# Output biases of five stages added by VectorE, and the expert biases in the middle of the last stage

## The chip, the core and the metric

One core of one Trainium2 chip runs the whole program. The metric is the device time of one execution in microseconds (us), the median of several runs. TensorE (PE) multiplies, with its weight loads shown apart (PEld); VectorE (DVE), ScalarE (ACT) and GpSimd (POOL) work on vectors; SyncE (SP) issues the transfers (DMA). Engines run their own instructions in order and wait for each other by semaphores.

## The reference

Four pre-norm layers over x of 2048 tokens x 128, in f32: eight stages, each of the form x = x + stage(layernorm(x)). Five of them matter here:

```python
# layer 0, attention: 16 heads of 8
q, k, v = split(x @ Wqkv.T + bqkv)
x = x + softmax(q k^T / sqrt(8)) v @ Wo.T + bo
# layer 0, feed-forward
x = x + gelu(h @ w1 + b1) @ w2 + b2
# layer 2, attention over three neighbouring tokens
x = x + out @ Wo.T + bo
# layer 3, feed-forward: eight experts, two per token, and a shared one
oe = silu((h @ w1 + b1) * (h @ w3 + b3)) @ w2 + b2      # per expert
x = x + sum(rw * oe) + (hs @ sw2 + sb2)
```

`bv` (the part of `bqkv` for v), `bo`, `b2`, `bo` and `sb2` are vectors of 128 that are added to every token. The expert biases `b2` of layer 3 (8 x 128) are weighted by the routing weights of the token.

## The kernel before

The running x lies in SBUF as `X`, 128 partitions x 16 tiles x 128: a token is a partition of a tile. Work goes in four chunks of four tiles (512 tokens; `NC`, `TPC`, `CW`). Every stage begins with a norm stage (VectorE normalizes tile by tile, TensorE transposes into `xnT`), during which SyncE issues the stage's weight loads. Each stage is a block: its engines start together and the next block starts when all are done.

A product whose result has tokens on partitions and features along the row can't take its bias from ScalarE's per-partition operand. The kernel before adds such a bias with a TensorE product over one row: `ones[0:1, 0:P]` (one partition of ones) times the bias row `[1, D]`, accumulated into the same PSUM tile. That is one such product for each of 16 tiles in each of five places:

- `l0_attend`, tasks of the kind "v" (L335, L336): the values of four chunks, written to PSUM `l0s_mx`, a ring of four buffers that also holds the maximum products (`max`, L346), the query and key products (`qk`, L331) and the output transposes (`ot`). ScalarE copies a values chunk from the ring to `V` (`fill_v`, L424); VectorE reduces the maximum products (L478). The table `DENSE0` puts chunk 0 ahead of the score loop and chunks 1 to 3 in its rounds 2, 3 and 4. A round is four scores (L362), four maximum products and sixteen value products (L376); there are 256.
- `token_major_out` (l0o; L581, L582): the output projection of the first attention. VectorE adds each chunk to `X` (L595) and computes the moments for the next norm (L156, L159), with the root steps (L168, L129 to L137) after the third and the fourth chunk.
- `l0_ffn` (l0f; L635 the bias, L637 four products): the downward product of a tile.
- `l2_attention` (l2a; L1250, L1251): the output projection, chunk by chunk between the score products (L1222), with one PSUM buffer `l2a_po`; VectorE adds at L1315.
- `l3_ffn` (l3f): here both kinds of bias come at the very end, for four chunks, in `biases(c)`: the expert biases as a product over eight rows (`maskT` times `b2`, L1643), the shared one over one row (L1644). They use the ring `l3f_dn` of two PSUM buffers, as the downward products of the experts do (L1634), which VectorE adds with the routing weight as its factor (L1767), or without one for the shared expert and the biases (L1763). The transposed routing weights `maskT` are made in the middle, behind groups 6, 8, 10 and 12 (`TURNED_AT`).

Of the kernel before, what the change touches and what calls it, by code (L numbers as in the profile page):

```python
# [10 lines left out]
ALU = mybir.AluOpType  # L11
# [4 lines left out]
P = 128  # L16
D = 128
# [51 lines left out]
def row_of(vector):  # L69

    return vector.rearrange("(a n) -> a n", a=1)

# [184 lines left out]
def l0_attend(nc, ctx, W, norm, xnT, vals, ident, ones, V, QS, KS):  # L257
# [38 lines left out]
    v_set, v_done = sem("v_set"), sem("v_done")  # L296
# [23 lines left out]
    with nc.Block() as block:  # L320
        @block.tensor
        def _(pe):
            def mx_task(key):
# [74 lines left out]
        def _(act):  # L398
# [22 lines left out]
            def fill_v(i):  # L421
                n = slot[("v", i)]
                act.wait_ge(mx_full, n + 1)
                nc.scalar.activation(V[:, TPC * i:TPC * (i + 1), :, 0:HD0],  # L424
                                     mx[:, n % MX0, :].rearrange("p (t j c) -> p t j c", t=TPC, c=HD0),
                                     ACT.Copy).then_inc(v_done, 1)
                act.wait_ge(v_done, i + 1)
                act.sem_inc(mx_free[n % MX0], 1)

# [6 lines left out]
            def fills(r):  # L436
                for kind, i in DENSE0.get(r, []):
                    if kind == "qk":
                        fill(i)
                    else:  # L440
                        fill_v(i)
# [4 lines left out]
            act.wait_ge(v_set, 2)  # L446
# [16 lines left out]
        def _(dve):  # L463
# [86 lines left out]
def token_major_out(nc, ctx, tag, W, w_dram, b_dram, vals, X, ident, ones, used, moments):  # L550
# [3 lines left out]
    bo = sb("bo", [1, D])  # L554
# [4 lines left out]
    transposed, copied, done, added = sem("transposed"), sem("copied"), sem("done"), sem("added")  # L559
    with nc.Block() as block:  # L560
        @block.sync
        def _(sp):
            sp.dma_start(Wo[:, :], w_dram).then_inc(loaded.sem, 16)
            sp.dma_start(bo[:, :], row_of(b_dram)).then_inc(loaded.sem, 16)
# [8 lines left out]
        def _(pe):  # L573
# [17 lines left out]
        def _(dve):  # L591
            for c in range(NC):
                dve.wait_ge(done, TPC * (c + 1))
# [10 lines left out]
def l0_ffn(nc, W, norm, X, xnT, ones, moments):  # L604

    NB = F0 // P
    with ExitStack() as ctx:
# [4 lines left out]
        b2 = sb("b2", [1, D])  # L612
        loaded = W["loads"].stage(4)

        def load(sp):
# [3 lines left out]
            sp.dma_start(b2[:, :], row_of(W["L0_ffn_b2"])).then_inc(loaded.sem, 16)  # L619
# [5 lines left out]
        up_done, act_done, dn_done, added = sem("up_done"), sem("act_done"), sem("dn_done"), sem("added")  # L625
        with nc.Block() as block:
            @block.tensor
            def _(pe):
                pe.wait_ge(loaded.sem, loaded.all)

                def down(c):
                    pe.wait_ge(act_done, NB * (c + 1))
                    for t in range(TPC * c, TPC * (c + 1)):
                        o = dn[:, c, (t % TPC) * D:(t % TPC + 1) * D]
                        nc.tensor.matmul(o, ones[0:1, 0:P], b2[0:1, :], start=True, stop=False)  # L635
                        for b in range(NB):
                            last = nc.tensor.matmul(o, hT[:, b, t * P:(t + 1) * P], w2[:, b, :],  # L637
                                                    start=False, stop=(b == NB - 1))
# [23 lines left out]
            def _(dve):  # L662
                for c in range(NC):
                    dve.wait_ge(dn_done, c + 1)
# [480 lines left out]
def l2_attention(nc, W, norm, X, xnT, ident, ones, moments):  # L1145
# [6 lines left out]
    with ExitStack() as ctx:  # L1152
# [4 lines left out]
        bo = sb("bo", [1, D])  # L1157
# [4 lines left out]
        def load(sp):  # L1162
# [4 lines left out]
            sp.dma_start(bo[:, :], row_of(W["L2_attn_bo"])).then_inc(loaded.sem, 16)  # L1167
# [22 lines left out]
        o_done, po_full, po_read = sem("o_done"), sem("po_full"), sem("po_read")  # L1190
# [1300 lines left out]
```

## Time and profile before

| | before |
|---|---|
| median of 3 runs | 3157.16 us (3152.45 to 3158.06) |
| profiled execution | 3151.58 us |
| its span, first to last instruction | 3149.8 us |
| TensorE busy | 2954.1 us, 94% |
| VectorE busy | 2210.3 us, 70% |
| ScalarE busy | 1419.3 us, 45% |
| mean granted clock of TensorE | 0.910 of 2.4 GHz |

Busy time is that of the whole program, over stages with different limits; the rows further down are from the places of the change. The granted clock has two levels, 1.0 (2.4 GHz) and 0.5 (1.2 GHz).

### The profile page before, as it was taken

To read this page: it belongs to the slowest core of one execution; us is meant where nothing else is said; L and a number is where in the kernel's file an instruction comes from. 1 tells how busy PE (TensorE), PEld (TensorE's weight loads), DVE (VectorE), ACT (ScalarE), POOL (GpSimd) and SP (SyncE) were. 2 spreads that over 40 slices of the span, in tenths; PEclk is the share of its full clock that TensorE was granted. 3 is DMA by queue.
4 is the path that set the end of the run, shared out by engine and by line. 5 is a ranking of instruction groups with operands and counts; after the bars stand their busy time and mean duration, and the time that the engine had idled before them with its cause. 6 is when DMAs were issued, how large, how long until landed. Compare 5 with 4: busy or idle time off the path is not lost. (4 is left out here: it accounts for less than half of the span.)

```text
span 3149.8 us, 43331 instructions
## 1 busy us (share of the span) xinstructions
PE 2954.1 (94%) x15864; PEld 1838.4 (58%) x15864; DVE 2210.3 (70%) x4583; ACT 1419.3 (45%) x2681; POOL 734.6 (23%) x608
## 2 busy tenths in 40 slices
PE   4999999999987999999999999999999787789799
PEld 2666666666654555555555555555554444556587
DVE  5788888888724877777877777777774637777554
ACT  1666666666641344444444444444444210322343
POOL 1000000000000244444444444444444100055200
PEclk7999999999987899999999999999999867555598
DMA  4112122121004011111111111111100100000000
GB/s 96 26 26 51 29 49 45 33 51 21 1 8 121 1 41 41 41 41 31 38 27 28 41 41 41 41 38 31 35 20 1 37 1 9 3 1 2 16 1 14
DMA packets 42128, 95.91 MB, mean 30 GB/s; under 512 B 12502, under 2 KB 31676, under 8 KB 32188
## 3 DMA queue, kind: packets, MB, share of 16 engines
q1 hardware_dynamic: 41916, 93.14, 13.0%
q8 instruction: 126, 2.06, 0.3%
q14 instruction: 86, 0.70, 0.1%
HBM read 35.18 MB, written 7.34 MB: 13 GB/s over the span
## 5 line engine op out<-in xcount | busy, mean ns | idle before, releaser
L957 ACT ACTIVATE l1a_PT<-l1a_st 128x512 f32<-128x512 f32 x1024 | 597.1, 598 | 759.6 <-PE l1a_st L873 755.5
L974 DVE TENSOR_REDUCE l1a_m<-l1a_aux 128x1 f32<-128x512 f32 x1024 | 667.6, 685 | 125.3 <-PE l1a_aux L835 123.1
L478 DVE TENSOR_REDUCE l0s_mquad<-l0s_mx 128x1 f32<-128x512 f32 x1024 | 635.5, 684 | 169.3 <-PE l0s_mx L346 169.3
L924 POOL TENSOR_TENSOR l1a_acc<-l1a_acc,l1a_PT 128x1024 f32<-128x1024 f32 x224 | 570.0, 2545 | 680.5 <-ACT l1a_PT L957 680.5
L454 ACT ACTIVATE l0s_PT<-l0s_st 128x512 f32<-128x512 f32 x1024 | 529.2, 601 | 236.0 <-PE l0s_st L362 232.6
L886 PE MATMUL l1a_ov<-l1a_PT,l1a_V 128*64 128x512 f32 x2048 | 495.7, 605 | 0.0
L871 PE MATMUL l1a_st<-l1a_QA,l1a_KA 128*128 128x512 f32 x1024 | 447.1, 437 | 2.4 <-issue 2.3
L362 PE MATMUL l0s_st<-l_QS,l_KS 128*128 128x512 f32 x1024 | 437.4, 430 | 3.6 <-ACT l0s_PT L454 3.5
L346 PE MATMUL l0s_mx<-l_KS,l_QS 120*128 120x512 f32 x1024 | 415.9, 412 | 20.4 <-DMA l_KS<-qk_rows 20.4
L873 PE MATMUL l1a_st<-l1a_QB,l1a_KB 65*128 65x512 f32 x1024 | 405.6, 396 | 0.0
L835 PE MATMUL l1a_aux<-l1a_KA,l1a_QA 128*128 128x512 f32 x1024 | 398.5, 437 | 0.8 <-DVE l1a_lo L986 0.8
L346 PEld LDWEIGHTS l0s_mx<-l_KS,l_QS 120*128 120x128 f32 x1024 | 328.5, 321 | 64.8 <-DMA l_KS<-qk_rows 22.0
L1022 DVE TENSOR_TENSOR l1a_acc<-l1a_acc,l1a_PT 128x1024 f32<-128x1024 f32 x224 | 272.7, 1217 | 91.0 <-ACT l1a_PT L957 91.0
L835 PEld LDWEIGHTS l1a_aux<-l1a_KA,l1a_QA 128*128 128x128 f32 x1024 | 200.7, 196 | 176.7 <-DVE l1a_m L974 82.0
L376 PE MATMUL l0s_ov<-l0s_PT,l_V 128*32 128x256 f32 x4096 | 274.1, 385 | 0.0
L886 PEld LDWEIGHTS l1a_ov<-l1a_PT,l1a_V 128*64 128x64 f32 x2048 | 124.2, 136 | 239.4 <-issue 177.6
L362 PEld LDWEIGHTS l0s_st<-l_QS,l_KS 128*128 128x128 f32 x1024 | 195.5, 192 | 114.2 <-ACT l0s_PT L454 87.1
L871 PEld LDWEIGHTS l1a_st<-l1a_QA,l1a_KA 128*128 128x128 f32 x1024 | 193.8, 189 | 109.5 <-issue 62.1
L913 POOL MEMSET l1a_KB<- 1x4096 f32 x1 | 3.5, 3504 | 942.9 <-POOLq L195 942.9
L873 PEld LDWEIGHTS l1a_st<-l1a_QB,l1a_KB 65*128 65x128 f32 x1024 | 193.6, 189 | 47.4 <-issue 13.4
L376 PEld LDWEIGHTS l0s_ov<-l0s_PT,l_V 128*32 128x32 f32 x4096 | 106.8, 109 | 103.9 <-issue 52.6
L1009 DVE SCALAR_TENSOR_TENSOR top_X<-l1a_aux,l1a_rinv,top_X 128x128 f32<-128x128 f32 x256 | 71.8, 344 | 54.5 <-PE l1a_aux L858 54.5
(348 smaller groups left out, 2763.7 us busy)
## 6 DMA issues: line engine op xcount, KB each, us to landing
l1a_KA<-l1a_hi SPq DMA_DIRECT2D x32, 512.0 KB, 7.9
l_QS<-qk_rows SPq DMA_DIRECT2D x64, 192.0 KB
l_KS<-qk_rows SPq DMA_DIRECT2D x64, 192.0 KB
l1a_QA<-l1a_hi SPq DMA_DIRECT2D x16, 512.0 KB, 4.5
l1a_QA<-l1a_lo SPq DMA_DIRECT2D x16, 512.0 KB, 8.6
l1a_QB<-l1a_hi SPq DMA_DIRECT2D x16, 512.0 KB, 4.5
l1a_KB<-l1a_lo SPq DMA_DIRECT2D x16, 512.0 KB, 6.4
qk_rows<-l0s_hi SPq DMA_DIRECT2D x64, 64.0 KB, 7.0
```

The costliest lines, as they stand in the source:

```text
L346: last = nc.tensor.matmul(o, q[:, tile, :], KS[r, h % BUF0, c * CW:(c + 1) * CW], start=True, stop=True)
L362: nc.tensor.matmul(st[:, b % ST0, :], KS[:, h % BUF0, kt * P:(kt + 1) * P], QS[:, h % BUF0, q:q + CW], start=True, stop=True).then_inc(st_ ...
L376: last = nc.tensor.matmul(ov[32 * q:32 * (q + 1), u % 2, :], V[:, u // 2, 2 * n + e, :], PT[:, (2 * r + e) % PT0, q // 2, at], start=(n == ...
L454: nc.scalar.activation(PT[:, g % PT0, b % 2, :], st[:, b % ST0, :], ACT.Exp).then_inc(exp_done, 1)
L478: nc.vector.tensor_reduce(mquad[:, u % 2, tile, g:g + 1], mx[:, n % MX0, :], axis=AX.X, op=ALU.max).then_inc(mx_free[n % MX0], 1)
L835: last = nc.tensor.matmul(o, QA[:, h % 3, q * P:(q + 1) * P], KA[:, h % 3, c * CW:(c + 1) * CW], start=True, stop=True)
L871: nc.tensor.matmul(st[:, u % ST1, :], KA[:, h % 3, kt * P:(kt + 1) * P], QA[:, h % 3, qc * CW:(qc + 1) * CW], start=True, stop=False)
L873: last = nc.tensor.matmul(st[:, u % ST1, :], KB[:, h % 2, kt * P:(kt + 1) * P], QB[:, h % 2, qc * CW:(qc + 1) * CW], start=False, stop=True)
L886: last = nc.tensor.matmul(ov[HD1 * (qc % 2):HD1 * (qc % 2) + HD1, qc // 2, :], V[:, h // 2 % 2, kt, HD1 * (h % 2):HD1 * (h % 2) + HD1], PT ...
L924: nc.gpsimd.tensor_tensor(acc[:, h % 2, 1, :], first, PT[:, g % PT_SLOTS, :], ALU.add).then_inc(added_pool, 1)
L957: nc.scalar.activation(PT[:, g % PT_SLOTS, (u % 2) * CW:(u % 2 + 1) * CW], st[:, u % ST1, :], ACT.Exp, scale=1.0 / float(np.sqrt(HD1))).th ...
L974: nc.vector.tensor_reduce(m4[:, b, q, c:c + 1], src, axis=AX.X, op=ALU.max).then_inc(aux_read, 1)
```

## The change

The bias tiles of the five places become `[128, 128]`, loaded with the row repeated over all partitions (64 KB in place of 0.5 KB each), and the one-row products go. In four stages VectorE adds the bias tile to `X` itself, four adds of 128x512 at the beginning of the stage's block (`add_bias`), before it adds the products. For the values, the evacuation of the PSUM ring moves from ScalarE to VectorE, which adds the bias tile in the same instruction and frees the buffer; it stands in VectorE's order where the chunk stands among the tasks. VectorE waits for the memset of `V` and for the bias load ahead of its first reduction. The expert biases become blocks of their own, of four 8-row products, in the groups 7, 9, 11 and 13 of the last stage.

```diff
+def add_bias(nc, X, bias, biased):
+    for c in range(NC):
+        x = X[:, TPC * c:TPC * (c + 1), :]
+        nc.vector.tensor_tensor(x, x, bias[:, :].unsqueeze(1).broadcast_to([P, TPC, D]), ALU.add).then_inc(biased, 1)
...
-    bv = sb("bv", [1, D])
+    bv = sb("bv", [P, D])
...
-        sp.dma_start(bv[:, :], row_of(W["L0_attn_bv"])).then_inc(b_loaded, 16)
+        sp.dma_start(bv[:, :], row_of(W["L0_attn_bv"]).broadcast_to([P, D])).then_inc(b_loaded, 16)
...
-                        nc.tensor.matmul(o[:, t * D:(t + 1) * D], xnT[:, at], Wt[:, 2, :], start=True, stop=False)
-                        last = nc.tensor.matmul(o[:, t * D:(t + 1) * D], ones[0:1, 0:P], bv[0:1, :],
-                                                start=False, stop=True)
+                        last = nc.tensor.matmul(o[:, t * D:(t + 1) * D], xnT[:, at], Wt[:, 2, :], start=True, stop=True)
...
-                        pe.wait_ge(v_done, u // (2 * TPC) + 1)
+                        n_v = slot[("v", u // (2 * TPC))]
+                        pe.wait_ge(mx_free[n_v % MX0], n_v // MX0 + 1)
...
             split_low(0)
+            dve.wait_ge(b_loaded, 32)
+            dve.wait_ge(v_set, 2)
...
+                elif kind == "v":
+                    dve.wait_ge(mx_full, n + 1)
+                    nc.vector.tensor_tensor(V[:, TPC * i:TPC * (i + 1), :, 0:HD0],
+                                            mx[:, n % MX0, :].rearrange("p (t j c) -> p t j c", t=TPC, c=HD0),
+                                            bv[:, :].rearrange("p (j c) -> p j c", c=HD0).unsqueeze(1)
+                                            .broadcast_to([P, TPC, J0, HD0]), ALU.add).then_inc(mx_free[n % MX0], 1)
...
-                nc.tensor.matmul(o, vT[:, t * P:(t + 1) * P], Wo[:, :], start=True, stop=False)
-                nc.tensor.matmul(o, ones[0:1, 0:P], bo[0:1, :], start=False, stop=True).then_inc(done, 1)
+                nc.tensor.matmul(o, vT[:, t * P:(t + 1) * P], Wo[:, :], start=True, stop=True).then_inc(done, 1)
...
+            dve.wait_ge(loaded.sem, loaded.all)
+            add_bias(nc, X, bo, biased)
             for c in range(NC):
+                dve.wait_ge(biased, c + 1)
                 dve.wait_ge(done, TPC * (c + 1))
...
-                        nc.tensor.matmul(o, ones[0:1, 0:P], b2[0:1, :], start=True, stop=False)
...
-                        nc.tensor.matmul(o, oT[:, t * P:(t + 1) * P], Wo[:, :], start=True, stop=False)
-                        last = nc.tensor.matmul(o, ones[0:1, 0:P], bo[0:1, :], start=False, stop=True)
+                        last = nc.tensor.matmul(o, oT[:, t * P:(t + 1) * P], Wo[:, :], start=True, stop=True)
...
-            downs_of[g] = range(len(downs), len(downs) + len(experts))
-            downs += [(y, c) for y in experts]
+            mine = [(y, c) for y in experts]
+            if g - 1 in TURNED_AT:
+                mine.append((N3, TURNED_AT.index(g - 1)))
+            downs_of[g] = range(len(downs), len(downs) + len(mine))
+            downs += mine
...
+                    if x == N3:
+                        pe.wait_ge(mt_read, c + 1)
                     for j in range(TPC):
                         o = dn[:, d % 2, j * D:(j + 1) * D]
+                        if x == N3:
+                            last = nc.tensor.matmul(o, maskT[:, TPC * c + j, :], b2[:, :], start=True, stop=True)
+                            continue
...
-                pe.wait_ge(mt_read, NC)
-                for c in range(NC):
-                    biases(c)
```

What stands in the engines' queues, at three places. TensorE before, from the first maximum products of the first attention over the values chunk 0 (in such rows `l_KS` and `l_QS` are keys and queries, `xN` a repetition):

```order
L346 MATMUL l0s_mx<-l_KS,l_QS 128x512 x28
L335 MATMUL l0s_mx<-l0s_W,top_xnT 128x128
L336 MATMUL l0s_mx<-l0s_bv,top_ones 128x128
L335 MATMUL l0s_mx<-l0s_W,top_xnT 128x128
L336 MATMUL l0s_mx<-l0s_bv,top_ones 128x128
```

The two products take turns four times. The same place on TensorE after the change, where line numbers have moved:

```order
L351 MATMUL l0s_mx<-l_KS,l_QS 128x512 x28
L342 MATMUL l0s_mx<-l0s_W,top_xnT 128x128 x4
L351 MATMUL l0s_mx<-l_KS,l_QS 128x512 x8
L338 MATMUL l0s_mx<-top_xnT,l0s_W 128x512 x2
L351 MATMUL l0s_mx<-l_KS,l_QS 128x512 x4
```

Four 128-row products stand in a row, and the one-row products are gone. VectorE at the beginning of l0o before the change (after the last work of the attention itself):

```order
L496 TENSOR_TENSOR l0a_vals<-l0s_mx,l0s_rden 128x2x4x8
L320 UNCONDITIONAL_BRANCH
L590 UNCONDITIONAL_BRANCH
L595 TENSOR_TENSOR top_X<-l0o_po,top_X 128x512
L156 BN_STATS top_stats<-top_X 128x6 x4
```

And VectorE at that place after it:

```order
L498 TENSOR_TENSOR l0a_vals<-l0s_mx,l0s_rden 128x2x4x8
L327 UNCONDITIONAL_BRANCH
L592 UNCONDITIONAL_BRANCH
L78 TENSOR_TENSOR top_X<-top_X,l0o_bo 128x512 x4
L600 TENSOR_TENSOR top_X<-l0o_po,top_X 128x512
L163 BN_STATS top_stats<-top_X 128x6 x4
```

Four adds out of SBUF have come ahead of the first add of a product; the rest of the stage is as it was. TensorE in a middle group of the last stage after the change, behind the upward products (`l3f_ab`) of group 8:

```order
L1635 MATMUL l3f_ab<-l3f_xl,l3f_wh 128x512
L1651 MATMUL l3f_dn<-l3f_w,l3f_hT 128x128 x16
L1648 MATMUL l3f_dn<-l3f_b,l3f_maskT 128x128 x4
L1673 MATMUL l3f_mt<-top_ident,l3f_mask 8x128 x4
L1635 MATMUL l3f_ab<-l3f_xh,l3f_wh 128x512
```

The line with `l3f_maskT` is a block of expert biases, which before stood, with the one-row products, behind the last downward product of the program.

## Rows read from the trace of the kernel before

**Rows 1.** The page, its first line.

```profile
span 3149.8 us, 43331 instructions
```

**Rows 2.** Busy us (instructions) by stretch: PE, PEld, DVE, ACT, POOL; clock; DMA; GB/s.

```profile
200.00:880.00 680.00, 678.31 (x5263) 467.14 (x5261) 540.62 (x931) 460.95 (x900) 0.00 (x0) 1.00 0.15 33
...
2540.00:2620.00 80.00, 58.85 (x150) 35.02 (x148) 30.72 (x92) 3.45 (x7) 0.00 (x0) 0.50 0.00 0
```

**Rows 3.** Timeline of the last 28 us: start, duration, engine, line, operation.

```profile
3124.15 7.31 PE L1634 MATMUL l3f_dn<-l3f_w,l3f_hT 128*128 128x128 f32 x64
...
3131.39 0.48 PE L1643 MATMUL l3f_dn<-l3f_b,l3f_maskT 8*128 8x128 f32 x2
3131.49 1.13 DVE L1767 SCALAR_TENSOR_TENSOR top_X<-l3f_dn,l3f_mask,top_X 128x128 f32<-128x128 f32 x4 [0.66 <-PE l3f_dn L1634]
...
3134.56 0.63 PE L1643 MATMUL l3f_dn<-l3f_b,l3f_maskT 8*128 8x128 f32 x2
...
3134.98 0.63 PE L1644 MATMUL l3f_dn<-l3f_sb,top_ones 1*128 1x128 f32 x2
...
3143.33 0.69 DVE L1763 TENSOR_TENSOR top_X<-l3f_dn,top_X 128x512 f32<-128x512 f32 x1 [2.72 <-PE l3f_dn L1644]
```

**Rows 4.** Timeline of TensorE, values chunk 1 of the first attention.

```profile
91.50 0.48 PE L336 MATMUL l0s_mx<-l0s_bv,top_ones 1*128 1x128 f32 x2
91.91 0.49 PE L335 MATMUL l0s_mx<-l0s_W,top_xnT 128*128 128x128 f32 x2
```

**Rows 5.** Timeline of TensorE, the first downward tile of l0f.

```profile
933.54 0.48 PE L635 MATMUL l0f_dn<-l0f_b,top_ones 1*128 1x128 f32 x2
933.95 1.16 PE L637 MATMUL l0f_dn<-l0f_w,l0f_hT 128*128 128x128 f32 x8
935.04 0.48 PE L635 MATMUL l0f_dn<-l0f_b,top_ones 1*128 1x128 f32 x2
```

**Rows 6.** Timeline around values chunk 0 of the first attention.

```profile
63.95 0.77 PE L335 MATMUL l0s_mx<-l0s_W,top_xnT 128*128 128x128 f32 x2
...
69.71 4.22 PE L346 MATMUL l0s_mx<-l_KS,l_QS 120*128 120x512 f32 x8
...
70.57 2.48 DVE L478 TENSOR_REDUCE l0s_mquad<-l0s_mx 128x1 f32<-128x512 f32 x4 [4.90 <-PE l0s_mx L346]
```

**Rows 7.** Timeline of l0o: first product, VectorE's chunks, its last instruction.

```profile
894.29 0.49 PE L581 MATMUL l0o_po<-l0o_Wo,l0o_vT 128*128 128x128 f32 x2
...
897.73 0.69 DVE L595 TENSOR_TENSOR top_X<-l0o_po,top_X 128x512 f32<-128x512 f32 x1 [5.58 <-PE l0o_po L582]
...
899.24 0.36 DVE L159 BATCH_NORM_AGGREGATE top_mv<-top_stats 128x2 f32<-128x6 f32 x4
...
908.99 0.69 DVE L595 TENSOR_TENSOR top_X<-l0o_po,top_X 128x512 f32<-128x512 f32 x1 [3.91 <-PE l0o_po L582]
...
912.13 0.17 DVE L137 SCALAR_TENSOR_TENSOR top_rstd<-top_work 128x12 f32<-128x12 f32 x1
...
917.96 0.16 DVE L137 SCALAR_TENSOR_TENSOR top_rstd<-top_work 128x4 f32<-128x4 f32 x1
```

**Rows 8.** Timeline at the start of the first attention.

```profile
30.59 0.53 POOL L505 MEMSET l_V<- 128x256 f32 x1
...
48.83 9.66 DVE L478 TENSOR_REDUCE l0s_mquad<-l0s_mx 128x1 f32<-128x512 f32 x16 [18.12 <-PE l0s_mx L346]
```

**Rows 9.** Timeline of l2a, six multiplications of 128x512 out of SBUF.

```profile
2531.75 3.70 DVE L1297 TENSOR_TENSOR l2a_prod<-l2a_q,l2a_k 128x512 f32<-128x512 f32 x6
```

**Rows 10.** DMA issues: KB each, median us from issue to landing.

```profile
l1a_bo<-in_L_attn_bo SPq DMA_DIRECT2D x1, 64.0 KB, 7.6
```

**Rows 11.** Timeline of l2a, output projection of chunk 0.

```profile
2558.63 0.79 PE L1250 MATMUL l2a_po<-l2a_Wo,l2a_oT 128*128 128x128 f32 x2
...
2564.42 5.30 PE L1222 MATMUL l2a_sc<-l2a_same_head,l2a_prod 128*128 128x16 f32 x24
2564.52 0.69 DVE L1315 TENSOR_TENSOR top_X<-l2a_po,top_X 128x512 f32<-128x512 f32 x1 [12.96 <-PE l2a_po L1251]
```

More of the change, by code:

```diff
@@ L295, in l0_attend @@
     heads_in = [sem(f"heads_in{i}") for i in range(BUF0)]
-    v_set, v_done = sem("v_set"), sem("v_done")
+    v_set = sem("v_set")
     m_done, m_placed = sem("m_done"), [sem(f"m_placed{i}") for i in range(2)]
@@ L553, in token_major_out @@
     Wo = sb("Wo", [P, D])
-    bo = sb("bo", [1, D])
+    bo = sb("bo", [P, D])
     vT = sb("vT", [P, S])
@@ L559, in token_major_out @@
     transposed, copied, done, added = sem("transposed"), sem("copied"), sem("done"), sem("added")
+    biased = sem("biased")
     with nc.Block() as block:
@@ L563, in _ @@
             sp.dma_start(Wo[:, :], w_dram).then_inc(loaded.sem, 16)
-            sp.dma_start(bo[:, :], row_of(b_dram)).then_inc(loaded.sem, 16)
+            sp.dma_start(bo[:, :], row_of(b_dram).broadcast_to([P, D])).then_inc(loaded.sem, 16)
             sp.wait_ge(loaded.sem, loaded.all)
@@ L611, in l0_ffn @@
         b1 = sb("b1", [P, NB])
-        b2 = sb("b2", [1, D])
+        b2 = sb("b2", [P, D])
         loaded = W["loads"].stage(4)
@@ L618, in load @@
             sp.dma_start(w2[:, :, :], W["L0_ffn_w2"].rearrange("(n p) d -> p n d", p=P)).then_inc(loaded.sem, 16)
-            sp.dma_start(b2[:, :], row_of(W["L0_ffn_b2"])).then_inc(loaded.sem, 16)
+            sp.dma_start(b2[:, :], row_of(W["L0_ffn_b2"]).broadcast_to([P, D])).then_inc(loaded.sem, 16)
         norm(load)
@@ L625, in l0_ffn @@
         up_done, act_done, dn_done, added = sem("up_done"), sem("act_done"), sem("dn_done"), sem("added")
+        biased = sem("biased")
         with nc.Block() as block:
@@ L634, in down @@
                         o = dn[:, c, (t % TPC) * D:(t % TPC + 1) * D]
-                        nc.tensor.matmul(o, ones[0:1, 0:P], b2[0:1, :], start=True, stop=False)
                         for b in range(NB):
                             last = nc.tensor.matmul(o, hT[:, b, t * P:(t + 1) * P], w2[:, b, :],
-                                                    start=False, stop=(b == NB - 1))
+                                                    start=(b == 0), stop=(b == NB - 1))
                     last.then_inc(dn_done, 1)
@@ L662, in _ @@
             def _(dve):
+                dve.wait_ge(loaded.sem, loaded.all)
+                add_bias(nc, X, b2, biased)
                 for c in range(NC):
+                    dve.wait_ge(biased, c + 1)
                     dve.wait_ge(dn_done, c + 1)
@@ L1156, in l2_attention @@
         Wo = sb("Wo", [P, D])
-        bo = sb("bo", [1, D])
+        bo = sb("bo", [P, D])
         same_head = sb("same_head", [P, P])
@@ L1189, in l2_attention @@
         p_done, tp_full, tp_read, dve_order = sem("p_done"), sem("tp_full"), sem("tp_read"), sem("dve_order")
[L1190 removed]
+        o_done, po_full, po_read, biased = sem("o_done"), sem("po_full"), sem("po_read"), sem("biased")
         XP, K, Q, V = range(4)
@@ L1286, in _ @@
                 dve.wait_ge(loaded.sem, loaded.all)
+                add_bias(nc, X, bo, biased)
                 for c in range(NC):
@@ L1313, in add @@
                     dve.wait_ge(po_full, c + 1)
+                    dve.wait_ge(biased, c + 1)
                     x = X[:, TPC * c:TPC * (c + 1), :].rearrange("p t d -> p (t d)")
@@ L1549, in l3_ffn @@
         b2 = sb("b2", [E8, D])
-        sb2 = sb("sb2", [1, D])
+        sb2 = sb("sb2", [P, D])
         expert_no = sb("expert_no", [P, E8])
@@ L1587, in l3_ffn @@
         ab_full, gate_done, z_done, h_done = sem("ab_full"), sem("gate_done"), sem("z_done"), sem("h_done")
-        dn_full, dn_read = sem("dn_full"), sem("dn_read")
+        dn_full, dn_read, shared_bias = sem("dn_full"), sem("dn_read"), sem("shared_bias")
         high_done, low_done = sem("high_done"), sem("low_done")
         groups = [(E8, c) for c in range(NC)] + [(2 * p, c) for p in range(PAIRS3) for c in range(NC)]
+        TURNED_AT = (6, 8, 10, 12)
         units, unit_of, downs, downs_of = [], {}, [], {}
@@ L1606, in block_before @@
         def block_before(d, c):
-            return max([i for i in range(d) if (downs + [(N3, k) for k in range(NC)])[i][1] == c], default=None)
+            return max([i for i in range(d) if downs[i][1] == c], default=None)
         with nc.Block() as block:
@@ L1635, in down @@
                                                     start=(i == 0), stop=(i == 1))
-                    last.then_inc(dn_full, 1)
-                def biases(c):
-                    d = len(downs) + c
-                    pe.wait_ge(dn_read, d - 1)
-                    for j in range(TPC):
-                        o = dn[:, d % 2, j * D:(j + 1) * D]
-                        nc.tensor.matmul(o, maskT[:, TPC * c + j, :], b2[:, :], start=True, stop=False)
-                        last = nc.tensor.matmul(o, ones[0:1, 0:P], sb2[0:1, :], start=False, stop=True)
                     last.then_inc(dn_full, 1)
@@ L1716, in _ @@
                 dve.wait_ge(loaded.sem, loaded.all)
+                add_bias(nc, X, sb2, shared_bias)
                 def wide(t):
@@ L1760, in add @@
                         dve.wait_ge(dn_read, before + 1)
+                    else:
+                        dve.wait_ge(shared_bias, c + 1)
                     if x >= E8:
@@ L1780, in _ @@
                     add(d, *downs[d])
-                for c in range(NC):
-                    add(len(downs) + c, N3, c)
 DM = 32
```

16 lines of the change are left out of this document (2 added, 14 removed).

## The prediction, made before the change was run

> **What bounds the kernel now.** I read the page first, then the clock and busy time by stretch, then the timeline of each of the five places that the diff touches, since a share of busy time over 3149.8 us says nothing of 25 us in one stage. The profiled execution took 3151.58 us, 1.8 around its span [rows 1]; the median of the three runs is 3157.16, 5.6 above it. In the long middle of the first attention TensorE is busy 678.3 of 680 us at the full clock [rows 2], so time that TensorE saves ahead of it moves everything behind it earlier. The reader should see in the rows one thing above all: what a one-row product costs beside a product over 128 rows.
>
> **The price of a bias product.** Every f32 product of 128 columns stands as two records. At the full clock (2.4 GHz), products of one shape follow each other every (3131.39 - 3124.15)/32 = 0.226 us [rows 3]; one change of shape lies in these 32, so I use 0.223. Where 128-row and one-row products take turns, each takes 0.41 us [rows 4], the 128-row ones too. In the feed-forward stage a bias product takes 933.95 - 933.54 = 0.41 and the four 128-row ones behind it 1.09, against 4 x 0.223 = 0.89 [rows 5]. So a change between a 128-row and a one-row product costs about 0.19 us in either direction, and a removed bias product gives back 0.223 + 2 x 0.19 = 0.61 us. At 1.2 GHz a product in turns takes (69.71 - 63.95)/8 = 0.72 us [rows 6], and one that follows its like 3134.98 - 3134.56 = 0.42 [rows 3] (8 rows and one row, which do not disturb each other); I use 0.43, so a change costs 0.29 there. That is the choice that makes this forecast: the 0.19 and 0.29 go away with the bias products, they are not a property of the 128-row product.
>
> The Trainium skill puts this as a rule in TensorEngine Tiling (Array Packing), Key Properties: changing the tiling mode (a product over at most 32 rows has one of its own) drains TensorE. It gives no figure. By its rule the extra 0.19 goes and the sum is the one below, 3104.8; without it the extra stays, which is rival 1, 3116.
>
> **First attention, values (four chunks).** Chunk 0 runs at 1.2 GHz: eight products, 5.76 us [rows 6]. Left are four at 0.43, with seven of eight changes gone: 5.76 - 4 x 0.43 - 0.29 = 3.8 us saved. VectorE sat idle 4.9 us for it [rows 6]; it now adds the bias itself (one PSUM read of 128x512, 0.69 us by the adds in [rows 7]), which fits into that idle time. Chunks 1 to 3 run at the full clock in a stretch where TensorE has no gaps [rows 4]: each loses 4 x 0.223 + 7 x 0.19 = 2.2 us, together 6.7. ScalarE's copy goes to VectorE, whose four reductions take 2.48 us [rows 6] of a round that the eight products had made 8 x 0.41 = 3.3 us longer. VectorE now waits at its start for the memset of the V tile and the bias load; the memset's last part starts at 30.59 and VectorE's first reduction at 48.83 after 18.1 us idle, behind a DMA [rows 8]: cost nothing, and if that cover were gone, the wait would be paid in full. **A: 10.5 us.**
>
> **First attention, output projection (l0o).** VectorE's chain: TensorE's first product at 894.29, first add at 897.73, end of the stage's chain at 917.96 + 0.16 = 918.12 [rows 7]. TensorE gives it 32 products. After the change it has 16, which even at 1.2 GHz take 16 x 0.43 = 6.9 us. So what is late next is VectorE: four bias adds of 128x512 out of SBUF, 3.70/6 = 0.62 us each [rows 9], 2.5 us, then two chunks of 899.24 + 0.36 - 897.73 = 1.9 us and two with the root steps of 912.13 + 0.17 - 908.99 = 3.3 us [rows 7]: 894.3 + 2.5 + 10.4 + 0.2 for hand-overs = 907.4. The bias load now writes 64 KB over 128 partitions in place of 0.5 KB, and both engines wait for it. Bounds of its delay: nothing, and the whole 7.6 us from issue to landing that a load of this same form took behind larger ones [rows 10]. Only 64 KB stand ahead of it here, so I take 0.4. End at 907.8. **B: 10.3 us.** It does not depend on the price of a change of rows.
>
> **First feed-forward (l0f).** Sixteen tiles of 1.50 us (933.54 to 935.04) [rows 5] become four products of 0.223 each, 0.89. TensorE has no gap there, and VectorE's adds lie far behind it. 16 x 0.61. The four SBUF adds (2.5 us) stand at the start, where VectorE has nothing to do until the first tiles are down. **C: 9.7 us.**
>
> **Third attention (l2a).** The whole stretch is at clock 0.50 [rows 2]. For each chunk TensorE starts the projection at 2558.63, VectorE waits 12.96 us and adds at 2564.52, 5.89 later [rows 11]; everything behind is VectorE's work and what waits for it. After: three products at 0.43, and from the last one's start to VectorE's what it was, 5.89 - 7 x 0.72 = 0.8: 2.1, so VectorE starts 3.8 earlier, and the products behind it 2564.42 - 2558.63 - 4 x 0.43 = 4.07. 3.9 on the chain, four chunks. **D: 15.6 us.** The bias adds stand ahead of VectorE's first read of the ring, in idle time.
>
> **Last feed-forward (l3f).** After the last expert add, at 3131.49 + 1.13 = 3132.62, the four bias blocks run until 3143.33 + 0.69 = 3144.02 [rows 3]: 11.4 us go from the end. Four blocks of four 8-row products come into the middle, each 4 x 0.223 + 2 x 0.19 = 1.28 us on a TensorE that has almost no gaps, 5.1 together. VectorE's share, one add of 0.69, lies beside them: an expert block takes TensorE 1.81 us and VectorE 1.13 [rows 3], so the ring of two PSUM blocks is free in time. **E: 6.3 us.**
>
> Sum: 10.5 + 10.3 + 9.7 + 15.6 + 6.3 = 52.4 us. 3157.2 - 52.4 = **3104.8** for the median (3099 for a profiled execution like the one shown).
>
> **Rivals.**
> 1. *The changes of rows still cost.* If a 128-row product of these stages keeps its 0.41 or 0.72 us: A 4 x 0.72 + 12 x 0.41 = 7.8, B 10.3, C 16 x 0.41 = 6.6, D 4 x 2.9 = 11.6, E 11.4 - 4 x 4 x 0.41 = 4.8; 41.1, so 3116. Against it: 128-row products in a row come every 0.22 [rows 3, 5]. 0.09.
> 2. *TensorE's clock rises in the third attention.* In the last stage the clock fell to 1.2 GHz while TensorE ran products of few rows without a gap [rows 3], so it may rise where they go; for the third attention the window has 0.50 [rows 2]. At 2.4 GHz TensorE's 58.9 - 15.6 us of work there would take half, 22 less; I estimate two thirds of it ahead of a waiting VectorE: 15, so 3090. Against it: TensorE's waits in that stretch stay, it is busy only 58.9 of 80 us [rows 2] and loses work. 0.08.
> 3. *The clock stays low in the first feed-forward,* because TensorE now idles while VectorE ends l0o. Its 64 products at 1.2 GHz cost 64 x 0.2 = 13 us; the upward ones have as many columns again, but part of them run at the low clock already, so I put 10: 3128. 0.06.
> 4. *Slower than before.* The values chunks' release moves from ScalarE to VectorE, in front of whose add up to four reductions stand. If TensorE waited for the ring and its clock fell to 1.2 GHz in the first attention, a round (24 matrix products, 5263/24 = 219 rounds in 680 us [rows 2], 3.1 us each) would take up to 3.1 us more. It ends slower from (52.4 + 6.3)/3.1 = 19 of 256 rounds at the low clock. Against it: a round with a values chunk leaves VectorE idle, and only four of 256 have one. With 20 rounds it gives 3167. 0.02.
>
> The Trainium skill, TensorE: Matmul & The Clock Gate, HAM oscillation, warns that gaps on TensorE bring the low clock, which speaks against a change that thins its work out. The trace agrees for the third attention only (clock 0.50 with TensorE idle 21 of 80 us [rows 2]); by the rule alone, rival 3 would be the forecast, 3128.
>
> **Numbers.** Forecast 0.73, the rivals as given (0.25), 0.02 for no difference (the stages' savings swallowed by waits that I don't see). The forecast's own range is 3099 to 3111: the clock's changes fall at other moments, 2 us at each of three stage starts, and the runs before spread by 5.6. To hold 8 in 10, with both neighbours at 3090 and 3116, the range is 3089 to 3118. 0.2% of this time is 6.3 us, about what a measurement of this kernel can tell from no change. Faster 0.96, same 0.02, slower 0.02.
>
> **What would show it.** In the changed kernel's trace: the sixteen tiles of l0f as one unbroken row of 128-row products, 0.89 us a tile; in l0o VectorE without idle time from the first bias add to the last root step, 13 us; the l2a add about 2.0 us behind the first projection product; the last feed-forward ending with an expert add; bias adds of 0.6 us each. The forecast is wrong if 128-row products alone still come every 0.41 us, if l0o's first product comes more than a microsecond later behind the load's issue than before, or if the clock's row differs in a stage that the diff does not touch.

## The result, and the profile after

The changed kernel takes 3102.1 us (median of 4 runs, 3100.95 to 3103.32); beside it on the same chip the kernel before took 3154.8 us (4 runs, 3147.02 to 3158.06). The ratio is 0.9837, with a 95% interval of 0.9817 to 0.9856. Forecast was 3104.8 us. The profiled span went from 3149.8 us [rows 1] to 3099.2.

The first lines of the page of the changed kernel (span; then busy time of each engine):

```profile
span 3099.2 us, 43036 instructions
PE 2896.3 (93%) x15704; PEld 1800.7 (58%) x15704; DVE 2224.9 (72%) x4603; ACT 1414.8 (46%) x2677; POOL 735.6 (24%) x608
```

The page's totals don't say where 50 us went. The stages do. In the table each length is the difference of two starts or ends read from the timelines: the first maximum's start; the last values' end; the first upward product of l0f; its last downward product's end; the first ring product of l2a; the end of its last product of the output projection; the first ab product of l3f; the end of the last instruction. "Rest" is what lies between l0f and l2a and between l2a and l3f, which the diff doesn't touch.

| us | to first maximum | L0 attention | l0o | l0f | l2a | l3f | rest |
|---|---|---|---|---|---|---|---|
| before | 48.8 | 843.3 | 32.2 | 40.2 | 96.6 | 178.3 | 1910.4 |
| after | 47.0 | 831.3 | 22.2 | 28.3 | 83.6 | 171.6 | 1915.1 |
| difference | -1.8 | -12.0 | -10.0 | -11.9 | -13.0 | -6.6 | +4.7 |
| forecast | 0 | -10.5 | -10.3 | -9.7 | -15.6 | -6.3 | 0 |

The values of the first attention, TensorE's timeline (start, duration; chunk 0, then chunks 1 and 2). A chunk's four products (two records each) have no bias products between them. At the full clock they take 1.05 us (chunks 1 and 2; chunk 0 runs at the half clock); before, with the bias products in turns, each of the eight products of chunk 1 took 0.41 [rows 4]:

```profile
62.15 2.06 PE L342 MATMUL l0s_mx<-l0s_W,top_xnT 128*128 128x128 f32 x8
...
83.61 1.05 PE L342 MATMUL l0s_mx<-l0s_W,top_xnT 128*128 128x128 f32 x8
87.61 1.06 PE L342 MATMUL l0s_mx<-l0s_W,top_xnT 128*128 128x128 f32 x8
```

The output projection l0o, timeline of all engines. The bracket is the engine's idle time before the row and what ended it. To be compared with [rows 7]:

```profile
879.06 0.41 SPq L567 DMA_DIRECT2D l0o_bo<-in_L_attn_bo  x1
...
881.95 2.50 DVE L78 TENSOR_TENSOR top_X<-top_X,l0o_bo 128x512 f32<-128x512 f32 x4 [3.61 <-DMA l0o_bo<-in_L_attn_bo]
...
881.97 3.84 PE L584 MATMUL l0o_po<-l0o_Wo,l0o_vT 128*128 128x128 f32 x32 [1.37 <-DMA l0o_bo<-in_L_attn_bo]
884.37 0.68 DVE L600 TENSOR_TENSOR top_X<-l0o_po,top_X 128x512 f32<-128x512 f32 x1
...
894.32 0.16 DVE L144 SCALAR_TENSOR_TENSOR top_rstd<-top_work 128x4 f32<-128x4 f32 x1
```

TensorE needs 3.84 us in place of some 20; VectorE's chain begins with the bias adds and ends at 894.48, 12.5 us later, with no bracket in between: VectorE has become this stage's bound. Both engines start only 2.9 us behind the load's issue.

The first downward block of l0f, the projection of l2a's chunk 0, and the last rows of l3f, again from the timeline, to be compared with [rows 5], [rows 11] and [rows 3]:

```profile
907.48 3.73 PE L642 MATMUL l0f_dn<-l0f_w,l0f_hT 128*128 128x128 f32 x32
...
2526.57 2.07 PE L1258 MATMUL l2a_po<-l2a_Wo,l2a_oT 128*128 128x128 f32 x8
...
2528.68 0.69 DVE L1324 TENSOR_TENSOR top_X<-l2a_po,top_X 128x512 f32<-128x512 f32 x1 [9.18 <-PE l2a_po L1258]
...
3092.30 1.13 DVE L1776 SCALAR_TENSOR_TENSOR top_X<-l3f_dn,l3f_mask,top_X 128x128 f32<-128x128 f32 x4 [0.66 <-PE l3f_dn L1651]
3093.71 0.40 SPq L124 DMA_DIRECT2D out_x<-top_X  x1
```

The sixteen products of a chunk of l0f (four tiles) stand in one row of 32 records, the next row starts at 911.05: 0.89 us a tile. In l2a the add follows 2.11 us behind the first product and VectorE waits 9.18 us for it, 3.8 less than before [rows 11]. The last stage ends with an expert add.

And one place that I had not looked at, the start of l3f, VectorE and GpSimd in the timeline:

```profile
2926.09 5.88 POOL L1684 TENSOR_TENSOR l3f_xl<-top_xnT,l3f_xh 128x512 fp32r<-128x512 f32 x4 [31.02 <-ACT l3f_xh L1690]
2927.51 5.62 DVE L78 TENSOR_TENSOR top_X<-top_X,l3f_sb 128x512 f32<-128x512 f32 x4 [3.55 <-DMA l3f_expert_no<-in_expert_no]
...
2933.05 1.47 DVE L1760 SCALAR_TENSOR_TENSOR l3f_z<-l3f_ab,l3f_b,l3f_gate 128x512 f32<-128x512 f32 x2
```

The four adds take 5.62 us here and not 2.5, and the first z comes 5.5 us behind the first ab product (3.8 before).

### The profile page after: what moved, and what is told of

It reads as the page before. It is cut to its first block and busy times, and to the rows that moved or that the text cites. A ratio compares the mean times of both kernels' runs of the same rounds, so it can differ in the third digit from the quotient of the medians.

```text
span 3099.2 us, 43036 instructions
## 1 busy us (share of the span) xinstructions
PE 2896.3 (93%) x15704; PEld 1800.7 (58%) x15704; DVE 2224.9 (72%) x4603; ACT 1414.8 (46%) x2677; POOL 735.6 (24%) x608
```

## Experiments

My theory of the gain: a 128-row product next to a one-row product costs a change of shape; the bias products' own columns are the smaller part. The rivals: the bias products cost only themselves; and, stage by stage, that part of the difference is the clock's, or that adds I called hidden are not. The first four experiments start from the kernel before, the others from the changed kernel.

**One: the same products over 128 rows.** The kernel before, with its bias products kept, over a tile that holds the bias in row 0 and zeros below.

```diff
-    bo = sb("bo", [1, D])
+    bo = sb("bo", [P, D])
...
-                nc.tensor.matmul(o, ones[0:1, 0:P], bo[0:1, :], start=False, stop=True).then_inc(done, 1)
+                nc.tensor.matmul(o, ones[:, 0:P], bo[:, :], start=False, stop=True).then_inc(done, 1)
```

> The kernel before with every bias product kept, but made over 128 rows in place of one, in the values of the first attention, its output projection, the first feed-forward part and the output projection of the third attention: the bias tile holds the bias in row 0 and zeros below, so the sums are the same. The last feed-forward part is untouched. My theory (the cost is the change between a 128-row and a one-row product, 0.19 us at the full clock and 0.29 us at the half clock, twice per bias product): about 6 us off in the values, 11 in the output projection of the first attention, 6.2 in the first feed-forward part (16 tiles by 0.39 us) and 9.4 in the third attention's, 32 us in all, so 3122 us, 3116 to 3128; down products of the first feed-forward part at 1.12 us for a tile of five. Rival (the cost is the bias product's own time, whatever its rows): within 3 us of the kernel before.

Measured: 3119.74 us (4 runs), ratio to the kernel before 0.9896 (0.9879 to 0.9912), where the kernel before took 3150.97 (9 runs): 33 us by the ratio, against 32 expected. By stages: attention 843.3 to 835.0, l0o 32.2 to 21.0, l0f 40.2 to 33.3, l2a 96.6 to 88.1: 8.3, 11.1, 6.9 and 8.5 us, where I expected 6, 11, 6.2 and 9.4, so the sum agrees better than its parts. The rival is out: of the 51 us of the whole change, about 33 come without removing a single product. Its l0f, TensorE's timeline:

```profile
911.40 0.38 PE L635 MATMUL l0f_dn<-l0f_b,top_ones 128*128 128x128 f32 x2
911.62 1.06 PE L637 MATMUL l0f_dn<-l0f_w,l0f_hT 128*128 128x128 f32 x8
912.51 0.39 PE L635 MATMUL l0f_dn<-l0f_b,top_ones 128*128 128x128 f32 x2
```

A tile takes 1.11 us (911.40 to 912.51), where it took 1.50 [rows 5]: 0.39 for two changes of shape. The remaining 0.22 is the product itself.

**Two and three: how many rows make a change.** The same kernel with the bias products over 64 and over 96 rows of that tile.

```diff
-                nc.tensor.matmul(o, ones[:, 0:P], bo[:, :], start=False, stop=True).then_inc(done, 1)
+                nc.tensor.matmul(o, ones[0:64, 0:P], bo[0:64, :], start=False, stop=True).then_inc(done, 1)
```

> As the kernel with 128-row bias products, but with 64 rows of the same zero-padded bias tile. Theory (any change of the number of rows costs TensorE its 0.17 to 0.29 us, whatever the number is): the four stages pace as in the kernel before; in the first feed-forward part the down products of chunk 1 begin 9.4 us behind those of chunk 0, and the span is near 3150 us. Rival (only products with few rows are set apart, and 64 rows go like 128): 7.9 us between these chunks, near 3117 us.

> As the kernel with 128-row bias products, but with 96 rows. Theory of classes (what counts is not the number of rows but whether they fit into a smaller part of the array: 96 rows need more than 64 and so the whole of it): like 128 rows, 7.9 us between the down products of chunks 0 and 1 of the first feed-forward part, span near 3117 us. Rival (any difference in rows costs): 9.4 us there, near 3150 us.

Measured, one run each: 3143.18 us with 64 rows, 3122.58 with 96; the kernel before took 3154.31 beside them. TensorE in l0f with 64 rows, then with 96:

```profile
925.55 0.49 PE L635 MATMUL l0f_dn<-l0f_b,top_ones 64*128 64x128 f32 x2
925.97 1.16 PE L637 MATMUL l0f_dn<-l0f_w,l0f_hT 128*128 128x128 f32 x8
927.05 0.48 PE L635 MATMUL l0f_dn<-l0f_b,top_ones 64*128 64x128 f32 x2
```

```profile
912.80 0.39 PE L635 MATMUL l0f_dn<-l0f_b,top_ones 96*128 96x128 f32 x2
913.03 1.06 PE L637 MATMUL l0f_dn<-l0f_w,l0f_hT 128*128 128x128 f32 x8
913.92 0.39 PE L635 MATMUL l0f_dn<-l0f_b,top_ones 96*128 96x128 f32 x2
```

A tile takes 1.50 us with 64 rows, exactly as with one, and 1.12 with 96, exactly as with 128. So it is not any difference in rows that counts, but on which side of a limit between 64 and 96 the number lies: 1 and 64 rows cost the change beside 128, 96 rows don't. Where between them the limit lies was not measured. The Trainium skill lists such classes in TensorEngine Tiling (Array Packing), Available Configurations: 128, 64 and 32 rows. The trace agrees that 64 and 128 are apart; that 96 rows go with 128 is this trace's finding (1.12 us a tile against 1.11). The page gives no price for a change; here it is 0.19 us.

Against my expectation the 64-row kernel was not at 3150: its l0o took 25.7 us in place of 32.2, with the same changes of shape. One row of the windows view (busy us of PE, PEld, DVE, ACT, POOL; granted clock) shows the difference, first of the kernel before, then of that with 64 rows:

```profile
896.00:910.00 14.00, 14.00 (x45) 9.80 (x44) 4.66 (x21) 0.00 (x0) 0.00 (x0) 0.57 0.00 0
```

```profile
896.00:910.00 14.00, 10.85 (x53) 7.63 (x52) 9.62 (x51) 0.00 (x0) 0.00 (x0) 1.00 0.00 0
```

With one row TensorE is busy without a gap at clock 0.57; with 64 rows the clock stays full until the stage's products are done. In experiment four, where l0o is as before, it is 0.51 there again. So with one-row products in turns the clock fell in both profiles, and with 64-row ones in the one profile that there is it did not; 6.5 of the 11.1 us that l0o gained with 128 rows came with 64 rows already, with the changes of shape all still there: they go with the clock. Whether the 64 rows kept the clock up, or the moment at which the stage began, one profile can't tell. So of the 33 us of experiment one not all is the direct price of the changes.

**Four: the bias of l0f alone.** The kernel before with only this stage's change.

```diff
-                        nc.tensor.matmul(o, ones[0:1, 0:P], b2[0:1, :], start=True, stop=False)
...
+                add_bias(nc, X, b2, biased)
```

> The kernel before with the bias of the first feed-forward part alone added by VectorE. My theory: 9.7 us off (16 tiles by 0.61 us), so 3145 us, and nothing added by the four adds, which lie under the up products; between 3142 and 3146. Rival (part of the 11.9 us by which this stage became shorter in the changed kernel came from the clock with which it began, and has nothing to do with its own bias): then the stage here gives 9.7 and not 11.9, because it still begins at the half clock. Against that, if the stage gives 11.9 us here too, the clock is no part of it.

Measured: 3139.96 us (6 runs), ratio 0.9967 (0.9955 to 0.9980), 10.4 us less. That is below the 3142 to 3146 that I expected, since the kernel before took 3151 us here and not 3155. The stage went from 40.19 to 30.47: 9.7, the forecast's term. So the further 2.2 us of the changed kernel are not this edit's. Its clock explains them: here the windows view has 0.50 for 910 to 925, and 0.95 for 925 to 945; in the changed kernel the whole stage is at 1.00:

```profile
900.00:925.00 25.00, 24.46 (x128) 16.84 (x129) 6.18 (x22) 12.03 (x18) 0.00 (x0) 1.00 0.00 1
```

**Five: the expert biases at the end again.**

```diff
-            if g - 1 in TURNED_AT:
-                mine.append((N3, TURNED_AT.index(g - 1)))
+            if g == len(groups) - 1:
+                mine += [(N3, k) for k in range(NC)]
```

> The changed kernel with the four expert-bias blocks at the end of the last stage again, as products over eight rows, in place of the middle. My theory (a block costs TensorE as much in the middle as at the end, so that the move alone is worth nothing, and the last stage's gain comes from the one-row products taken out): within 1 us of the changed kernel, 3101 to 3104 us. The bias blocks at the end take about 4.4 us there and leave out the same in the middle. Rival (at the end a block is paid in full, while in the middle it fills idle time of TensorE): 4 to 5 us slower than the changed kernel, 3106 to 3108.

Measured: 3105.57 us (4 runs, 3094.34 to 3107.75), ratio 0.9856 (0.9839 to 0.9872). The times don't settle it: the interval overlaps the changed kernel's. The stage does: from the first ab product to the last z 154.4 us in place of 159.1, and from there to the end 17.3 in place of 12.5: -4.7 and +4.7. The end of that kernel in the timeline:

```profile
3080.84 5.24 PE L1648 MATMUL l3f_dn<-l3f_b,l3f_maskT 8*128 8x128 f32 x32
...
3086.12 0.69 DVE L1772 TENSOR_TENSOR top_X<-l3f_dn,top_X 128x512 f32<-128x512 f32 x1 [1.22 <-PE l3f_dn L1648]
```

The move is worth nothing in the stage (171.6 us in both kernels), as expected: a block costs TensorE as much in the middle as at the end. What the last stage gained, it gained from the one-row products.

**Six: the adds of l3f later.** Each chunk's bias is added just ahead of its first product add.

```diff
-                add_bias(nc, X, sb2, shared_bias)
...
+                        nc.vector.tensor_tensor(xb, xb, sb2[:, :].unsqueeze(1).broadcast_to([P, TPC, D]),
+                                                ALU.add).then_inc(shared_bias, 1)
```

> The changed kernel with the four adds of the shared bias in the last stage moved from its start to just ahead of each chunk's first product add, out of the stretch in which GpSimd copies beside them. There they took 5.62 us together, 1.4 us each, against 0.62 us each in the first attention's output projection. My theory (VectorE and GpSimd slow each other there, and the adds delay the first gated product by 1.7 us): the adds take about 0.62 us each in their new place, the first z comes about 3.8 us behind the first product in place of 5.5, and the stage becomes up to 1.7 us shorter, 3100 to 3102 us. Rival (the delay is absorbed by buffers ahead of TensorE, or is paid again in the add's new place): no change of the time, 3102 us, although the adds are faster.

Measured: 3098.09 us (4 runs, 3097.72 to 3103.18), ratio 0.9829 (0.9813 to 0.9846), not told apart from the changed kernel by its time. VectorE and GpSimd in its timeline:

```profile
2927.00 4.97 POOL L1684 TENSOR_TENSOR l3f_xl<-top_xnT,l3f_xh 128x512 fp32r<-128x512 f32 x4 [31.02 <-ACT l3f_xh L1690]
```

```profile
2932.28 0.75 DVE L1758 SCALAR_TENSOR_TENSOR l3f_z<-l3f_ab,l3f_b,l3f_gate 128x512 f32<-128x512 f32 x1 [7.42 <-ACT l3f_gate L1704]
...
2946.13 0.68 DVE L1768 TENSOR_TENSOR top_X<-top_X,l3f_sb 128x512 f32<-128x512 f32 x1
```

Half of the theory holds. Away from each other GpSimd's four pieces take 4.97 us (5.88 beside the adds), an add 0.68 (1.64 to 1.77 beside them), and the first z comes 3.84 us behind the first ab product in place of 5.5. But from the first ab product to the last z it takes 160.4 us in place of 159.1. The adds now stand in front of the search for the experts (the mask is complete 24.2 us behind the first ab product, 23.5 in the changed kernel). Both halves of the rival are right: the late first z had cost nothing, as experiment five shows too (154.4 us with the slow adds at the start, 154.3 in the kernel before without any), and in their new place the adds cost 1.3 us, of which the later mask may be 0.7; the rest was not traced. The start, where the adds are slow, was the cheaper place.

**Seven, eight and nine: the changed kernel again; l0o's load and adds earlier; that together with the late adds of l3f.** In eight and nine, the weights and bias of l0o are loaded with the attention's own, and the bias is added in an idle stretch of VectorE in the attention's tail.

```diff
+                    if i == UNITS0 - 1:
+                        dve.wait_ge(bo_loaded, 32)
+                        add_bias(nc, X, bo, o_biased)
```

> The changed kernel as it is, for a comparison with the three others on the same chip: 3102 us, 3099 to 3105.

> The changed kernel with the weights and the bias of the first attention's output projection loaded with the attention's own loads, and with its four bias adds put into VectorE's work for the attention's last group, ahead of a wait in which VectorE stood idle. Theory: the chain of VectorE in this projection begins with its first product add, without the load behind it (which ended 2.9 us behind its issue) and without 2.5 us of bias adds: 3 to 4 us off, 3098 to 3099 us. Rival (the adds in the attention's tail delay a reduction there that gates its last products): the gain at the projection is given back in the tail, within 1 us of the changed kernel.

> The early loads and adds of the first attention's output projection and the late adds of the last stage together: the two gains add up, 4 to 5 us below the changed kernel, 3097 to 3098 us, if both theories hold; if the late adds were worth nothing, the same time as with the early loads alone.

Measured, five runs each on one chip: the changed kernel 3102.43 us, ratio 0.9843 (0.9829 to 0.9856); early 3097.26, 0.9836 (0.9822 to 0.9849); both 3101.49, 0.9840 (0.9827 to 0.9853), where I expected the two gains to add up to 3097 to 3098. By time alone no difference is shown. The timeline of the early kernel:

```profile
865.39 2.49 DVE L78 TENSOR_TENSOR top_X<-top_X,l0a_bo 128x512 f32<-128x512 f32 x4
```

```profile
882.40 3.74 PE L582 MATMUL l0o_po<-l0a_Wo,l0o_vT 128*128 128x128 f32 x32
883.49 0.69 DVE L595 TENSOR_TENSOR top_X<-l0o_po,top_X 128x512 f32<-128x512 f32 x1 [3.20 <-PE l0o_po L582]
```

The attention takes 831.4 us as in the changed kernel, so the adds cost nothing in its tail, and l0o takes 19.5 us in place of 22.4 (19.4 in the kernel with both). The 2.9 us are real in the stage. In the early kernel l0f then took 30.4 us, in that with both 28.3, and in the second run of the changed kernel, in which no instruction differs from the first, 29.7 where the first had 28.3. Such shifts of the clock, of 1 to 4 us in several stages, are as large as what this edit gives. So I don't claim a faster kernel, only a shorter stage. With both, the late adds of l3f cost 1.3 us of l3f (173.0 against 171.7) as in experiment six.

**Ten: hidden adds twice.** The bias adds of l0f and l2a are made twice.

```diff
                 add_bias(nc, X, b2, biased)
+                dve.wait_ge(biased, NC)
+                add_bias(nc, X, b2, again)
```

> The changed kernel with the bias adds of the first feed-forward part and of the third attention's output projection made twice, so that these two biases stand doubled in the output; eight adds more, about 5 us of VectorE's time. Theory (they lie under the up products and under the first projection products, so their price is nothing): within 1 us of the changed kernel, and the first product add of the third attention's projection begins as before or at most 0.5 us later. Rival (the adds were already on the path there): 2 to 5 us slower.

Measured: 3101.27 us (4 runs, 3094.06 to 3103.57), ratio 0.9837 (0.9822 to 0.9852): no slower. l0f took 28.26 us, as in the changed kernel; l2a 81.4, as in the second run of the changed kernel. These adds are free where they stand.

## Why the prediction was right

**The price of a bias product** was the step on which most rested, and it held: 0.61 us at the full clock splits into 0.39 for two changes of shape (experiment one) and 0.22 for the product. At 1.2 GHz, from the starts of l2a's chunks 0 and 1: 19.98 us apart before, 17.89 with 128-row bias products, 16.19 after. Divided by a chunk's eight changes and four products this is 0.26 us for a change (I had 0.29) and 0.43 for a product (0.43). Rival 1 fell with it. One step of the working was loose: with one change of shape taken off, [rows 3] give (7.24 - 0.19)/32 = 0.220 us for a product and not the 0.223 that I used; l0f then showed 0.223 (3.57 us for sixteen), so it did no harm.

**A, values**: forecast 10.5, measured 12.0. Chunks 1 to 3 came as computed, 2.2 us closer to each other (6.24 apart before, 4.00 after), and what follows chunk 3 another 1.8 closer. From chunk 0 to chunk 1 it was 5.8 and not 3.8, and the difference goes with the clock: after chunk 0 it rose at 66.4 us and not at 78.8. The windows view of 66 to 77, before and then after:

```profile
66.00:77.00 11.00, 10.90 (x24) 6.40 (x23) 5.06 (x9) 1.28 (x2) 0.00 (x0) 0.50 0.34 73
```

```profile
66.00:77.00 11.00, 9.59 (x27) 5.68 (x26) 9.65 (x17) 6.51 (x10) 0.00 (x0) 0.98 0.24 53
```

This came back in every profile: the rise is at 77.1 to 78.8 us in the three kernels with one-row or 64-row products here, and at 65.7 to 68.8 in the eight others. The kernel with 96 rows stands between them: full from 67.8 to 71.2, low again, and full for good from 74.6. It has no changes of shape, so their absence alone does not fix the moment. I had watched for a clock that falls where TensorE thins out, and not for one that rises where the changes of shape go. The first maximum came 1.8 us earlier, but in the second run of the changed kernel at 48.7, so this is no effect of the change. Rival 4 did not come: the clock was full from 66.4 to 889.0 us.

**B, l0o**: forecast 10.3, measured 10.0. Two misses work against each other. The wider load held the first product back to 2.91 us behind its issue (1.43 before): 1.5 us where I took 0.4. That is beyond the microsecond that I had named as a sign of being wrong, so this sign came. Against that, the chain from the bias adds to the last root step took 12.5 us and not 13.1: a chunk took 1.78 (884.37 to 886.15) and not 1.9, since the rows overlap, which a sum of durations does not see. In the kernel before nothing waited for the load: TensorE came to the first product straight from its transposes. In experiment one it waited for a contiguous 64 KB load, 1.84 us behind its issue. The two timelines, before and experiment one:

```profile
892.46 1.94 PE L575 MATMUL l0o_tp<-top_ident,l0a_vals 128*128 128x128 f32 x16 [0.82 <-PEq L320]
892.86 0.26 SPq L564 DMA_DIRECT2D l0o_bo<-in_L_attn_bo  x1
```

```profile
882.66 0.41 SPq L564 DMA_DIRECT2D l0o_bo<-in_L_attn_bo  x1
884.50 0.49 PE L581 MATMUL l0o_po<-l0o_Wo,l0o_vT 128*128 128x128 f32 x2 [0.31 <-DMA l0o_bo<-in_L_attn_bo]
```

So about 1.1 of the 1.5 us are the repeating of one row over the partitions (2.91 against 1.84), and l0o gained 11.1 in experiment one with all products kept. With the load where it stands, the 128-row product was the better way for this stage (21.0 us against 22.2); with load and adds taken out of the stage, as in experiment eight, VectorE's way is the shorter one (19.5).

**C, l0f**: forecast 9.7, and by itself exactly that (experiment four). The 11.9 of the changed kernel contain 2.2 of the clock: rival 3, a clock that stays low here, had the sign wrong. The clock fell in l0o at 889.0 for 10.2 us and was up again at 899.2, ahead of the first upward product at 900.54; before, it was low until 928.7. TensorE had been idle since 885.8 and stayed so until 895.4. By the Trainium skill, TensorE: Matmul & The Clock Gate, HAM oscillation, such a gap brings the low clock, and it did. What I had not thought of is that the kernel before already had the low clock here, from 898.0 to 928.7, and that the fall of the changed kernel could be over in time. With the load earlier (experiment eight) it was over at 904.1, 4.3 us into the stage, and l0f took 2.1 us more: rival 3 in small.

**D, l2a**: forecast 15.6, measured 13.0, and 15.2 in the second run of the changed kernel. The chain by chunks is the term: chunks 0 and 1 came 3.8 us closer (3.9 forecast), and the add stands 2.11 us behind the product (2.1). The 2.2 us that are missing in the first profile stand ahead of it. 1.8 of them are in the first eight ring products, which ran in part at the half clock in the first profile and at the full one in the second:

```profile
2486.12 5.51 PE L1220 MATMUL l2a_ring<-top_xnT,l2a_w 128*128 128x512 f32 x8 [0.93 <-PEq L202]
```

```profile
2490.02 3.67 PE L1220 MATMUL l2a_ring<-top_xnT,l2a_w 128*128 128x512 f32 x8 [0.93 <-PEq L202]
```

In experiments six and nine the stage took 84.2 us with these eight at 3.67, so the place of the loss moves from kernel to kernel. The four adds were free (experiment ten). The term's mechanism was right; I had left the clock at a stage's start in the range and not in the sum. Rival 2 did not come: the clock was at 0.50 again from 2506.9 to 2578.6, over all four projections.

**E, l3f**: forecast 6.3, measured 6.6. The part at the end came out at 11.4 us (from 23.96 to 12.54 behind the last z), the part in the middle at 4.8 (154.3 to 159.1 from the first ab product to the last z) where I had 5.1: a block takes TensorE 1.08 us (2992.41 to 2993.49). Wrong was "bias adds of 0.6 us each": three of the four here took 1.64 to 1.77 us, because I had not looked at who else works at that moment. It cost nothing only because the late first z was absorbed. The Trainium skill, SBUF: State Buffer, SBUF: two separate sides, has a port pair that an operation of VectorE with two SBUF inputs and one of GpSimd that reads SBUF can't hold at once: the first to start has it for its whole length and the other waits. The rows agree in that both grew, but unequally: three adds lost 1.0 us each, GpSimd 0.9 us in all.

**The rest**: forecast 0, measured +4.7 us in stages that the diff doesn't touch. In the three kernels with one-row or 64-row products in l2a and the attention it was 1910.1 to 1911.1 us, in the nine others 1910.6 to 1917.5, and 1915.1 and 1916.9 in the two profiles of the changed kernel. The granted clock goes with it: in the five profiles with up to 1911.8 us of rest it was at the half level for 386 to 391 us of it, in the seven with 1914.3 us or more for 394 to 402 (before 388.7, after 401.9). So the clock's row differs in stages that the diff does not touch, the third of my signs of being wrong. What shifted it was not shown, and why the shift is seldom to the good stays open.

So 52.4 forecast and 50.6 of span measured: the mechanism right in all five, the terms off by 1.5 (A), 0.3 (B), 2.2 (C), 2.6 (D) and 0.3 us (E), the larger ones by the moment at which the clock changed. That the total came within 2 us is in part luck: A, C and E gave 4.0 more than forecast and the first maximum 1.8, B and D 2.9 less, and the rest took back 4.7; and in B two misses, of 1.1 and 0.6 us, work against each other.

## What to carry to other kernels

Look for products of few rows between products of many: at the full clock each pair of changes cost 0.39 us, nearly twice the product itself. If the small product must stay, fill it up with zeros to 128 rows; that alone gave 33 of 51 us here (96 rows 32 us, in one run), and in l0o, where VectorE is the next bound, it was the better way as long as the adds and their load stayed in the stage. When work moves to an engine "in idle time", look who else is busy in that moment; and where stages end in waits, judge an edit of 3 us by its stage in two profiles and not by the total.

## What the runs showed of the hardware

A change between 64 and 128 rows costs TensorE as much as one between 1 and 128, and one between 96 and 128 nothing: a tile of l0f took 1.50 us with bias products of 1 and of 64 rows, 1.12 with 96 and 1.11 with 128. TensorE's clock fell in l0o while one-row and 128-row products took turns without a gap (two profiles; in a third, with 64-row products, it did not), and it rose 8 to 13 us later in the first attention in the three profiles where products changed shape (77.1 to 78.8 us against 65.7 to 68.8 in eight without such changes; 74.6 with 96 rows). An add of 128x512 out of two SBUF operands took 1.64 to 1.77 us beside a GpSimd operation of the same shape, and 0.68 without; the GpSimd piece took up to 1.74 in place of 1.28. A 64 KB load that repeats one row over 128 partitions landed 2.91 us behind its issue, a contiguous one of 64 KB at the same place 1.84, and nothing waited for the 0.5 KB row, which was there 1.43 us behind its issue at the latest (all three measured to the first product; 2.91 to 2.96 in five profiles, 1.84 to 2.02 in three, 1.43 and 1.48 in two).
